# Two load buffers per matrix, their loads on ACT's queue, and w_down's quantization moved into the first FFN

## What is computed

```python
def _weight_quant(w):
    scale = 1.0 / jnp.clip(jnp.mean(jnp.abs(w)), 1e-05)
    return jnp.clip(jnp.round(w * scale), -1.0, 1.0) / scale
def _act_quant(x):
    scale = 127.0 / jnp.clip(jnp.max(jnp.abs(x), axis=-1, keepdims=True), 1e-05)
    return jnp.clip(jnp.round(x * scale), -128.0, 127.0) / scale
def _bitlinear(x, w):
    return jnp.einsum('bsi,oi->bso', _act_quant(x), _weight_quant(w))
def ffn(x, w_gate, w_up, w_down):      # w_gate, w_up: 4096 x 1024, w_down: 1024 x 4096
    return _bitlinear(silu(_bitlinear(x, w_gate)) * _bitlinear(x, w_up), w_down)

x = x + 0.5 * ffn(layernorm(x), ...)   # FFN1
x = x + attention(layernorm(x), ...)   # 16 heads, 4 key/value groups, causal
x = x + 0.5 * ffn(layernorm(x), ...)   # FFN2
```

## Time and profile before

| | |
|---|---|
| median of 2 runs | 4870.06 us (4865.56 to 4874.55) |
| profiled execution, own time | 4879.18 us |
| its span on the slowest core | 4877.2 us |
| spans of the other seven cores | 4842.1 to 4855.6 us |
| granted TensorE clock, mean | 0.807 to 0.811 on all cores |
| DMA, mean over the span | 119 GB/s |

### The profile page before, as it was taken

One profiled execution on the slowest core, in us unless ns is written; L12 is line 12 of the kernel. 1 busy time (PEld: TensorE's weight loads), 2 busy tenths in 40 slices (PEclk: granted clock), 3 DMA queues, 4 the chain that ended last, 5 costly groups with the idle time before them and its releaser, 6 DMA issues.

```text
span 4877.2 us, 40940 instructions; the slowest of 8 cores (4842.1 to 4877.2 us)
## 1 busy us (share of the span) xinstructions
PE 2069.2 (42%) x9644; PEld 858.9 (18%) x9644; DVE 1791.6 (37%) x2475; ACT 732.6 (15%) x759; POOL 271.2 (6%) x372
## 2 busy tenths in 40 slices
PE   0000000000728373857507688854073543628377
PEld 0000000000313131323203233321031221203132
DVE  1226232130171726350122333213826455472800
ACT  5200025000101010100000566630010100101000
POOL 1001000001100010101000000000000000001000
PEclk9999999999969696988758555557587776869689
DMA  8648646632323232489843000034222222313588
GB/s 267 183 128 283 147 143 215 140 89 90 133 78 113 86 119 88 124 187 202 185 111 66 6 1 1 1 96 167 71 98 78 87 87 78 112 60 112 137 197 210
DMA packets 481678, 582.65 MB, mean 119 GB/s; under 512 B 348321, under 2 KB 355489, under 8 KB 473250
## 3 DMA queue, kind: packets, MB, share of 16 engines
q0 software_dynamic: 82688, 331.37, 21.6%
q1 hardware_dynamic: 365056, 140.58, 14.2%
q10 hardware_dynamic: 33698, 108.09, 6.3%
HBM read 364.97 MB, written 133.17 MB: 102 GB/s over the span
## 4 chain that ended last, share of the span: by engine, by line
DMA 33%; PE 26%; DVE 26%; issue 7%; ACT 5%; SPq 2%; DVEq 1%; ACTq 0%; POOLq 0%; POOL 0%
PE pu L576 8%; PE pg L563 7%; DMA wsl<-tuT 7%; ACT strips L842 4%; PE app L830 3%; DVE fqh L620 3%; DVE t1h L623 3%; DVE ast L594 3%; DMA xst<-x1h 3%; DMA q2t<-q2h 3%; DMA tt_q<-tu_nat 3%; DMA wds<-tdT 2%; DMA tt_q<-td_nat 2%; DMA tt_q<-tg_nat 2%; PE pd L664 2%
## 5 line engine op out<-in xcount | busy, mean ns | idle before, releaser
L563 PE MATMUL pg<-wsl,q1t 128*128 128x512 bf16 x2048 | 519.5, 400 | 1264.9 <-ACT sg L572 485.3
L576 PE MATMUL pu<-wsl,q1t 128*128 128x512 bf16 x2048 | 527.1, 404 | 185.0 <-DMA wsl<-tuT 185.0
L585 DVE TENSOR_TENSOR hb<-sg,pu 128x512 f32<-128x512 f32 x256 | 176.0, 688 | 935.7 <-PE pu L576 912.0
L563 PEld LDWEIGHTS pg<-wsl,q1t 128*128 128x128 bf16 x2048 | 208.7, 102 | 1538.8 <-issue 1323.4
L572 ACT ACTIVATE sg<-pg,sgv 128x512 f32<-128x512 f32 x256 | 175.9, 687 | 1569.5 <-PE pg L563 890.9
L664 PE MATMUL pd<-wds,q2t 128*128 128x512 bf16 x1024 | 280.0, 418 | 233.4 <-DMA wds<-tdT 181.3
L842 ACT ACTIVATE strips<-app,sc 128x1024 bf16<-128x1024 f32 x320 | 339.3, 1111 | 204.3 <-PE app L830 167.9
L830 PE MATMUL app<-qfm,kfm 64*128 64x512 bf16 x640 | 297.4, 584 | 76.8 <-ACT strips L842 54.4
L379 PE MATMUL pmisc<-onesf,asum_q 128*1 128x1 f32 x6 | 0.6, 163 | 739.1 <-DVE asum_q L377 739.1
L576 PEld LDWEIGHTS pu<-wsl,q1t 128*128 128x128 bf16 x2048 | 206.1, 102 | 469.1 <-issue 263.1
L323 DVE SCALAR_TENSOR_TENSOR qna<-fqa,t1a 128x1024 bf16<-128x1024 f32 x32 | 39.2, 1226 | 383.4 <-DMA q1h<-qna 378.7
(11 more groups left out here) (109 smaller groups left out, 2040.6 us busy)
## 6 DMA issues: line engine op xcount, KB each, us to landing
wsl<-tgT POOLq DMA_DIRECT2D x64, 1024.0 KB, 7.7
wsl<-tuT POOLq DMA_DIRECT2D x64, 1024.0 KB, 5.8
wds<-tdT POOLq DMA_DIRECT2D x64, 1024.0 KB, 7.7
wst<-wg POOLq DMA_DIRECT2D x32, 1024.0 KB, 9.5
wst<-wu POOLq DMA_DIRECT2D x32, 1024.0 KB, 9.0
wst<-wd POOLq DMA_DIRECT2D x32, 1024.0 KB, 8.1
q2h<-fqh ACTq DMA_DIRECT2D x32, 1024.0 KB, 3.9
xst<-x1h ACTq DMA_DIRECT2D x32, 512.0 KB, 4.0
```

The source lines that it names most:

```text
L563: mk(P, "tensor", lambda e, f=f, sp=sp, j4=j4, s=sg_slot: e.matmul(pg[sp][:], q1t[:, f, j4 * 128:(j4 + 1) * 128], wsl[s][:, f, :], start=( ...
L576: mk(P, "tensor", lambda e, f=f, sp=sp, j4=j4, s=su_slot: e.matmul(pu[sp][:], q1t[:, f, j4 * 128:(j4 + 1) * 128], wsl[s][:, f, :], start=( ...
L585: mk(P, "vector", lambda e, sp=sp, j4=j4, n=n: e.tensor_tensor(hb[:, j4, n * 512:(n + 1) * 512], sg[sp][:], pu[sp][:], ALU.mult), reads=[b ...
```

## The change

- `quant_matrix` has two `wst` buffers per matrix and not four shared by all: `wst_g`, `wst_u` of 128 x 2048, `wst_d` of 128 x 1024. Scales, partial sums and the columns of `pmisc` are per matrix too.
- g's loads are issued by POOL as before; those of u and d by ACT (`queue="scalar"`).
- `tnb` is the same buffer as `mbuf`, so the combining instruction writes over its input.
- d goes in 32 blocks of 128 x 1024, by column blocks first, and not in 16 of 128 x 2048.
- A transposing load depends on the stores of its own columns and rows of `nat`, not on all of them; the order on SP is still stores first within one call of `pass2`.
- d's pass 2 and its transposes are left out of the preparation. The callback `ffn1_mid_cb` emits them in the first FFN in two halves, of 16 blocks and 16 transposes each: behind phase1(1) and behind phase1(2).
- The layer norm has two `xst` buffers, the load of tile i+2 is emitted behind the subtraction of tile i (L300), and `q1h` is stored by ACT's queue.
- `pbuf`, `mbuf`, `ttmp` and `wst_d` stay allocated through the first FFN. The matmul banks of that FFN wait for the last uses of `pmisc`.

The diff, cut to its core:

```diff
-        xst = [sb(f"xst{i}", [128, C]) for i in range(3)]
+        xst = [sb(f"xst{i}", [128, C]) for i in range(2)]
...
-                sx = ln_rot[0] % 3
+                sx = ln_rot[0] % 2
...
             for i, j in enumerate(tl):
-                if i + 2 < len(tl):
-                    load(i + 2)
...
                     lnb[s][:], xst[sx][:], mv[:, 0:1], ALU.subtract),
                     reads=[b_xst[sx], b_mv], writes=[b_lnb[s]])
+                if i + 2 < len(tl):
+                    load(i + 2)
...
-                t_q1h.append(mkdma(P, "sync", q1h[j * 128:(j + 1) * 128, :], qna[s][:], reads=[b_qna[s]]))
+                t_q1h.append(mkdma(P, "scalar", q1h[j * 128:(j + 1) * 128, :], qna[s][:], reads=[b_qna[s]]))
...
+        pbuf = sbr("pbuf_q", [128, 2048], BF16)
+        mbuf = sbr("mbuf_q", [128, 2048], BF16)
+        tnb = mbuf
+        ttmp = sbr("tt_q", [128, 2048], BF16)
...
+        b_tnb = b_mbuf
...
+        wstq = {"d": [sbr(f"wst_d{i}", [128, 1024]) for i in range(2)]}
...
+        for m in "gu":
+            wstq[m] = [stu.enter_context(nc.sbuf_tensor(f"wst_{m}{i}", [128, 2048], F32, side="right"))
+                       for i in range(2)]
...
+        def quant_matrix(name, w_in, nat, tT, rows, cols, route="act",
+                         queue="gpsimd", defer_p2=False, chunk_w=2048):
+            bw = min(cols, chunk_w)
+            a = chunk_w // bw
...
-                for rb in range(nrb):
-                    for hc in range(ncc):
+                for hc in range(ncc):
+                    for rb in range(nrb):
...
-                s = i % 4
+                s = i % 2
                 dst = wst[s][:] if a == 1 else wst[s][:].rearrange("p (a c) -> p a c", a=a)
-                mkdma(P, "gpsimd", dst, ap, writes=[b_wst[s]])
+                mkdma(P, queue, dst, ap, writes=[b_wst[s]])
...
+            def cover_hi(f, hh):
+                hc_t = (f * 128) // bw
+                return hc_t * nrb + ((hh + 1) * rh) // rpb
+
+            def pass2(lo=0, hi=nblk):
+                for i, ap, napw in blocks():
+                    if not (lo <= i < hi):
+                        continue
+                    s = i % 2
...
+                    mkdma(P, queue, dst, ap, writes=[b_wst[s]])
+                    if route == "act":
+                        mk(P, "scalar", lambda e, s=s: e.activation(
+                            pbuf[:, 0:chunk_w], wst[s][:], AF.Sign, scale=swv[name][:], bias=bm05[:]),
+                            reads=[b_wst[s], b_swv[name]], writes=[b_pbuf], extra=b_bm05.rdeps())
+                        mk(P, "scalar", lambda e, s=s: e.activation(
+                            mbuf[:, 0:chunk_w], wst[s][:], AF.Sign, scale=swv[name][:], bias=bp05[:]),
+                            reads=[b_wst[s], b_swv[name]], writes=[b_mbuf], extra=b_bp05.rdeps())
+                        mk(P, "vector", lambda e: e.scalar_tensor_tensor(
+                            tnb[:, 0:chunk_w], pbuf[:, 0:chunk_w], -1.0, mbuf[:, 0:chunk_w],
+                            ALU.mult, ALU.subtract),
+                            reads=[b_pbuf], writes=[b_tnb])
...
+                    state["nat"][i] = mkdma(P, "sync", napw, srctn, reads=[b_tnb])
+                state["done"] = max(state["done"], hi)
+                while state["tp"] < len(trans) and cover_hi(*trans[state["tp"]]) <= state["done"]:
...
+                    mkdma(P, "sync", tsl, nat[hh * rh:(hh + 1) * rh, f * 128:(f + 1) * 128],
+                          writes=[b_ttmp[hb_]], extra=cdeps, transpose=True)
                     mkdma(P, "sync", tT[f * 128:(f + 1) * 128, hh * rh:(hh + 1) * rh],
                           tsl, reads=[b_ttmp[hb_]])
+                return P.qcover("sync")
+            if defer_p2:
+                return pass2, nblk
+            return pass2()
...
+        t_tgT = quant_matrix("g", wg_in, tg_nat, tgT, INNER, C, queue="gpsimd")
+        ln_toks = emit_ln(x_in, range(0, 4))
+        finish_is1(range(0, 4))
+        t_tuT = quant_matrix("u", wu_in, tu_nat, tuT, INNER, C, route="dve", queue="scalar")
+        ln_toks += emit_ln(x_in, range(4, 10))
+        finish_is1(range(4, 10))
+        d_p2, d_nblk = quant_matrix("d", wd_in, td_nat, tdT, C, INNER, queue="scalar",
+                                    defer_p2=True, chunk_w=1024)
+        ln_toks += emit_ln(x_in, range(10, 16))
+        finish_is1(range(10, 16))
+        mid1()
...
+        def ffn1_mid_cb(gi):
+            if gi == 1:
+                d_p2(0, d_nblk // 2)
+            elif gi == 2:
+                tern_done["d"] = d_p2(d_nblk // 2, d_nblk)
...
                 phase1(0)
+                if mid_cb:
+                    mid_cb(0)
                 phase1(1)
+                if mid_cb:
+                    mid_cb(1)
                 phase1(2)
+                if mid_cb:
+                    mid_cb(2)
                 for g in range(NG):
                     if g + 3 < NG:
                         phase1(g + 3)
```

More of the change, by code:

```diff
@@ L339, in finish_is1, with sbr @@
                     reads=[b_rstd], writes=[b_is1])
-        def quant_matrix(qb, name, w_in, nat, tT, rows, cols, route="act"):
-            bw = min(cols, 2048)
-            a = 2048 // bw
+        st2q = top.enter_context(contextlib.ExitStack())
+        def sbr(name, shape, dt=F32):
+            return st2q.enter_context(nc.sbuf_tensor(name, shape, dt, side="right"))
+        pmisc_rws = {m: RW() for m in "gud"}
+        pbuf = sbr("pbuf_q", [128, 2048], BF16)
+        mbuf = sbr("mbuf_q", [128, 2048], BF16)
@@ new lines, in build_program @@
+        tnb = mbuf
+        ttmp = sbr("tt_q", [128, 2048], BF16)
+        tot = sbr("tot_q", [1, 4])
+        onesrow = sbr("or_q", [1, 128])
+        b_onesrow = RW(); b_pbuf = RW(); b_mbuf = RW()
+        b_tnb = b_mbuf
+        b_ttmp = [RW(), RW()]
+        b_tot = {m: RW() for m in "gud"}
+        mk(P, "vector", lambda e: e.memset(onesrow[:], 1.0), writes=[b_onesrow])
+        partq = {m: sbr(f"part_{m}", [128, 1]) for m in "gud"}
+        asumq = {m: sbr(f"asum_{m}", [128, 1]) for m in "gud"}
@@ L378, in quant_matrix @@
                     reads=[b_part], writes=[b_asum])
-            mk(P, "tensor", lambda e: e.matmul(pmisc[0:1, 0:1], asum[:], onesf[:], start=True, stop=True),
+            c0, c1 = 2 * mi, 2 * mi + 1
+            mk(P, "tensor", lambda e: e.matmul(
+                pmisc[0:1, c0:c0 + 1], asum[:], onesf[:], start=True, stop=True),
                 reads=[b_asum, b_onesf], writes=[pmisc_rw])
             mk(P, "vector", lambda e: e.tensor_scalar(
[L382 to L386, removed]
+                tot[0:1, mi:mi + 1], pmisc[0:1, c0:c0 + 1], 1.0 / (rows * cols), 1e-5, ALU.mult, ALU.max),
+                reads=[pmisc_rw], writes=[b_tot[name]])
+            mk(P, "tensor", lambda e: e.matmul(
+                pmisc[:, c1:c1 + 1], onesrow[:], tot[0:1, mi:mi + 1], start=True, stop=True),
+                reads=[b_onesrow, b_tot[name]], writes=[pmisc_rw])
+            mk(P, "vector", lambda e: e.reciprocal(swv[name][:], pmisc[:, c1:c1 + 1]),
                 reads=[pmisc_rw], writes=[b_swv[name]])
@@ L389, in quant_matrix @@
             mk(P, "vector", lambda e, msc=msc: e.tensor_single_scalar(
[L390 removed]
+                meanv[name][:], pmisc[:, c1:c1 + 1], msc, ALU.mult),
                 reads=[pmisc_rw], writes=[b_meanv[name]])
[L392 to L405, removed]
[L406 to L419 removed]
@@ L420, in quant_matrix @@
-            nat_cover = P.qcover("sync")
             rh = min(rows, 1024)
             nhalf = rows // rh
-            ti = 0
-            for f in range(cols // 128):
-                for hh in range(nhalf):
-                    hb_ = ti % 2
-                    ti += 1
+            trans = [(f, hh) for f in range(cols // 128) for hh in range(nhalf)]
+            state = {"nat": [None] * nblk, "done": 0, "tp": 0, "ti": 0}
+            rpb = 128 * a
+            def cover_hi(f, hh):
+                hc_t = (f * 128) // bw
+                return hc_t * nrb + ((hh + 1) * rh) // rpb
@@ L518, in emit_ffn @@
                 b_pg = [RW(), RW()]; b_pu = [RW(), RW()]; b_pd = [RW(), RW(), RW(), RW()]
+                for rwb in b_pg + b_pu + b_pd:
+                    rwb.r += list(psum_guard)
                 if pre_q1 is None:
@@ L919, in build_program @@
             else:
[L920 removed]
+                emit_ffn(1, x_in, x1h, pre_q1=pre1,
+                         mid_cb=ffn1_mid_cb, psum_guard=pmisc_guard)
+                st2q.close()
                 P.fence()
```

111 lines of the change are left out of this document (52 added, 59 removed).

## The result

| | before | after |
|---|---|---|
| median | 4872.63 us (8 runs) | 5107.72 us (9 runs) |
| profiled execution | 4879.18 us | 5097.11 us |
| span of its slowest core | 4877.2 us | 5095.5 us |
| first matmul of FFN1 | 1225 us | 1037 us |

The changed kernel is slower: 1.0475 times the time before, 95% interval 1.0454 to 1.0496. The forecast was slower by 140 us, with a range up to 5095 us; the medians differ by 235 us, the two profiled executions by 218. The 17 us between the two differences are spread of the runs that no row explains.

What follows compares the result with a forecast made beforehand. It took the serial preparation, ordered by SP and DVE, and then FFN1's phase boundaries to bound the kernel. Preparation -224, boundaries +370 and FFN2 -6 gave +140 on 4870, so 5010 us, range 4930 to 5095.

Steps and rivals of the forecast that it cites:

- g's transposes: Preparation: 32 transposing loads, 135 us before, slowed by u's pass-1 loads beside them by 25 us to 160.
- d pass 1: Preparation: 32 blocks of 512 KB on ACT's queue, one load in flight, 4.8 us each, 154 us; bounds 131 and 198.
- g pass 1, scale, pass 2: Preparation: loads with two buffers 82 us, scale 2, then stores 10.0 us apart because of the alias, 160 us.
- u pass 2: Preparation: 16 stores after g's transposes, 7.95 us apart with the comparison in series, 130 us; bounds 125 to 143.
- end of the preparation: Sum of the preparation's terms to mid1's end: 994 us against 1218, so -224 us; bounds -293 and -114.
- PE gap after group 1: FFN1: PE waits for d's stores, transposes and then q1t, 267 us where 91 stood.
- FFN2, earlier q1t: FFN2: with q1h stores off SP, q1t comes early and PE fills its banks before silu: -6 us (0 to -10).
- The rival on collisions: Pass-1 loads of u and d slow the transposes fully, boundaries reach 212 each: 5180, anything over 5095 counted; chance 0.08.
- The boundaries: FFN1 after groups 1 and 2: d's deferred work uncovered, 185 us per boundary, 370 for two; bounds 350 and 424.
- the two loops that I gave: d's pass 2 in FFN1: Sign, combining and store, 4.9 us; load plus Sign, 5.3 on alternate blocks; 5.2 taken.
- One sign of being wrong: Listed as showing the forecast wrong: transposes of 5 us and more throughout.
- That d's work might be off PE's path: Rival: deferred blocks done in idle gaps of DVE and ACT inside groups, costing 0 to 50, time 4646 to 4700; chance 0.07.

Runs made afterwards that it cites:

- e4: The kernel before with one edit, the q1h stores issued by ACT and not by SP: 4755.5 us, ratio 0.9772.
- e3: The changed kernel with u's 16 pass-1 loads issued by SP, so they start after g's transposes: 5116.54 us, ratio 1.0512.
- e5: The kernel before with q1h stored by ACT and the pass-1 loads of u and d issued by SP, behind the transposes: 4715.37 us, ratio 0.967.
- e6: The changed kernel with the 32 loads of d's pass 1 issued by POOL and not by ACT: 5062.08 us, ratio 1.0385.
- e7: The changed kernel with a separate buffer for the combined values of g and u, d keeping the alias: 5011.91 us, ratio 1.0277.
- e1: The changed kernel with the q1t loads waiting on the last matmul of the group before alone, not all 512: 5048.63 us, ratio 1.0371.
- e9: The changed kernel with d's pass 2 and transposes spread inside groups 1 and 2, pass 2's loads issued by POOL: 4729.08 us, ratio 0.9697.

## Why the prediction was wrong in size

The sign, the mechanism and the order of the parts were right. Two terms of the sum were too small, g's transposes beside u's loads (160 us, measured 206) above all, and then d's pass 1. One cost was missing, the 512 waits ahead of q1t (27 us at each of two boundaries). From the profiled executions:

| term | predicted, us | measured, us |
|---|---|---|
| g pass 1, scale, pass 2 | 247 | 230 |
| g's transposes | 160 | 206 |
| u pass 2 | 130 | 128 |
| norm, six tiles | 64 | 63 |
| d pass 1 | 154 | 167 |
| norm, six tiles | 71 | 69 |
| mid1 | 168 | 166 |
| end of the preparation | 994 | 1029 |
| PE gap after group 1 | 267 | 282 |
| PE gap after group 2 | 267 | 287 |
| FFN2, earlier q1t | -6 | +2 |

**The transposes beside u's loads** (term "g's transposes", 160 us, bounds 135 and 185). This is the step that failed furthest: 206 us lies outside its bounds. I bounded the collision by the whole of u's pass 1, 50 us, and reasoned that the two DMA shares would fit side by side (122 us of 135). The transposes were 71 us longer and not 25, and in e4 each pass of 50 us cost 76 and 96. Shares of busy time didn't add that way: the share rose to 0.89, and 0.89 x 206 is 183 us of busy engines where I had added up 122. The bytes in that stretch, 39 MB at 190 GB/s, were only a fifth more than the 33 MB of the two stretches that I added. Why transposes and large loads take so much more engine time together stays open.

The rival on collisions drew on the Trainium skill, DMA: Bandwidth & Descriptors, section Issuing engines are not separate DMA queues, which says that DMAs started by different engines run on the same 16 DMA engines. e3 agrees: apart the two took 220 us, side by side 206. e4 and e5 show a loss beyond it. The same section of the Trainium skill says that a second issuing engine saves only the time to issue. The measurement differs where a transfer stands unissued in an engine's order: moving the small q1h stores to ACT's queue was worth 111 us (e4).

**d pass 1** was mis-sized by 13 us: 5.2 us a block and not 4.8, from a landing of 4.9 beside the transposes. The mechanism, one load in flight, is shown by the wait of Abs on 32 loads and by e6.

**g pass 1 and pass 2** were 17 us too dear. With two in flight a 1 MB load of g landed in 5.8 us (median), where I had taken some 7. The stores came 9.9 us apart against 10.0, but only 15 such spacings lie between 16 stores, and I had counted 16 and 3 us more.

**u pass 2** came out right by luck. Its stores were 8.5 us apart (127.64 by 15) and not 7.95, and again 15 spacings stood where I had counted 16 and 3 us more. (6.57 + 1.28 is 7.85, besides.) So the alias cost more at u than I had it: by e7's rows 34 us at g and 37 at u, 71 together, against (10.0 - 7.7) x 16 = 37 and (7.95 - 6.57) x 16 = 22, 59 together, in the sum.

**The boundaries.** Terms: the first store 100 us after PE's stop (predicted 97), stores 83 (83), transposes 60 (67), q1t 12 (20), and 27 us of waits that were not in the sum. I wrote that SP issues q1t behind the transposes, and counted each DMA that it issues, but not the 512 waits that it has to pass first. Each is a row of its own in the trace of before, at a place where they cost nothing. e1 shows them: 22 and 28 us of the gaps, 51 us of the time. The block period was 5.3 to 5.5 us (predicted 5.2). Of the two loops that I gave, it is the one of load and Sign, at every block and not at alternate ones, so here too one load is in flight. ACT after; a load (ACTq) is issued just ahead of the second Sign, and the next first Sign waits for it:

```profile
1538.64 1.24 ACT L450 ACTIVATE pbuf_q<-wst_d,bm,swv_d 128x1024 bf16<-128x1024 f32 x1 [2.92 <-DMA wst_d<-wd]
1539.74 0.33 ACTq L54 DMA_DIRECT2D wst_d<-wd  x1
1539.79 1.23 ACT L453 ACTIVATE mbuf_q<-wst_d,bp,swv_d 128x1024 bf16<-128x1024 f32 x1
1543.97 1.24 ACT L450 ACTIVATE pbuf_q<-wst_d,bm,swv_d 128x1024 bf16<-128x1024 f32 x1 [2.96 <-DMA wst_d<-wd]
```

My bounds for the two boundaries, 350 and 424, are wider than the blocks' bounds of 78 and 101 give (360 and 406), and hold the 405.

**FFN2**: q1t did come early, but silu waited for the scales, not for PE; the first silu starts 23 us after the last norm tile's result is begun, and 21 before.

Together: -224 became -189 (35 us), 2 x 185 became 405 (35), -6 became +2 (8). 140 + 78 = 218, as between the profiled executions. The rest to the 235 of the medians stays open.

**The signs.** The first matmul (1037 us), the spacing of g's stores (9.9) and DVE's missing wait on q1h were as I had said; d's blocks (5.2) and the gaps (282 and 287) were above. One sign of being wrong did show: transposes of 5 us and more. g's took 6.4 us each (206 by 32) and u's 5.4 (171 by 32), d's in FFN1 3.8.

What I had named as the rivals: the measured 5108 lies in the one on collisions, which began at 5095. It was the right one in kind, with about half the extra time of its limit of 5180. But at g its limit, the whole load time of 50 us, was too low: 71 were measured. That d's work might be off PE's path was wrong for this kernel and right for e9: the idle time I pointed at (DVE and ACT inside the groups) is real, and only the order of emission kept the work out of it.

## What to carry to other kernels

Work moved out of a serial preparation has to be emitted inside the stretch where its engines idle, in small pieces: that cost 31 us here. How large a piece may be no run tried. Between two phases at which every engine hands over to the next, it was paid in full, 410 us. Ahead of such a move, list everything that stands behind it in each engine's order, satisfied waits included. And check what a transfer stands behind before giving it more company: moving the small q1h stores out of a long queue won 111 us here, while large loads beside transposes won 18 us (two in flight, e3) or lost 50 (four, e5).

## What the hardware showed that I had not expected

- A satisfied semaphore wait on SP cost about 53 ns: 512 of them took 27.1 us, in the changed kernel and in e9.
- A transposing load of 256 KB landed in 3.5 us without large loads and in 8.4 us (medians) beside two 1 MB loads in flight. With four in flight, the transposes of one matrix took 211 to 235 us in place of 135 to 139, so 76 to 96 us for loads that take 45 us apart.
- Sign after silu needed no table load, nor silu after Sign: in FFN1 after, no such row stands between the first silu and the end of d's pass 2.
